# First attention of a two-block transformer on one core: joined maxima for one query tile in eight, outputs kept by channel, one bias product, a new opening

## The reference

```python
q = _rope(proj(Wq, bq)); k = _rope(proj(Wk, bk)); v = proj(Wv, bv)   # 16 heads of 16
scores = jnp.einsum('bhtd,bhsd->bhts', q, k) / scale                 # 2048 x 2048 a head
attn = jax.nn.softmax(scores, axis=-1)
out = jnp.einsum('bhts,bhsd->bhtd', attn, v)
out = out.transpose(0, 2, 1, 3).reshape(Bb, Tt, C)
return jnp.einsum('btc,oc->bto', out, Wo) + bo
```

## Time and profile before

| what | value |
|---|---|
| three runs | 3234.95 us median (3229.55 to 3236.52) |
| the profiled execution: span | 3219.8 us, 15.15 us under that median |
| PE busy | 3012.8 us (94%) |
| DVE busy | 2490.0 us (77%) |
| ACT busy | 2268.6 us (70%) |
| POOL busy | 780.4 us (24%) |
| mean granted PE clock | 0.964 |

### The profile page before, as it was taken

How to read it: one execution, slowest core, us unless ns; L and a number is a source line. 1 busy time by engine, 2 the same in 40 slices (tenths; PEclk the granted TensorE clock), 3 DMA queues, 4 the chain that set the end, 5 groups by cost and what they waited for, 6 DMA issues and landing times. The chain is left out here.

```text
span 3219.8 us, 63296 instructions
## 1 busy us (share of the span) xinstructions
PE 3012.8 (94%) x23672; PEld 1873.1 (58%) x23672; DVE 2490.0 (77%) x4820; ACT 2268.6 (70%) x4998; POOL 780.4 (24%) x1019
## 2 busy tenths in 40 slices
PE   8969999999999999999985999999999999999995
PEld 5733333333333333333354788888888888888884
DVE  4668899999989999899445767677777767777774
ACT  3407788888878888788875767676667767676663
POOL 4510000000000000000054434343434434343432
PEclk9958999999989999999997999999999999999998
DMA  3333212333322233322040000000000000000002
GB/s 115 112 82 41 38 25 41 41 41 41 41 32 32 40 41 41 41 41 41 12 161 23 1 1 0 0 0 0 0 1 35 1 1 0 0 0 0 0 1 71
DMA packets 47115, 99.37 MB, mean 31 GB/s; under 512 B 17184, under 2 KB 29472, under 8 KB 40480
## 3 DMA queue, kind: packets, MB, share of 16 engines
q1 hardware_dynamic: 42400, 95.48, 15.6%
q10 hardware_dynamic: 4544, 1.38, 0.2%
HBM read 71.13 MB, written 25.69 MB: 30 GB/s over the span
## 5 line engine op out<-in xcount | busy, mean ns | idle before, releaser
L691 DVE TENSOR_REDUCE mx<-aux 128x1 f32<-128x1024 f32 x1024 | 1246.5, 1224 | 116.4 <-PE aux L556 108.8
L661 ACT ACTIVATE probs<-scores 128x512 f32<-128x512 f32 x2048 | 1118.5, 597 | 250.1 <-PE scores L580 143.2
L556 PE MATMUL aux<-k_stack,q_stack 48*128 48x512 f32 x2048 | 792.8, 466 | 27.7 <-DMA k_stack<-qk_dram 19.5
L580 PE MATMUL scores<-q_stack,k_stack 50*128 50x512 f32 x2048 | 777.8, 456 | 13.4 <-ACT probs L661 13.4
L592 PE MATMUL pv<-probs,v_ones 128*32 128x256 f32 x8192 | 670.2, 400 | 0.1
L580 PEld LDWEIGHTS scores<-q_stack,k_stack 50*128 50x128 f32 x2048 | 317.3, 189 | 439.5 <-ACT probs L661 414.7
L592 PEld LDWEIGHTS pv<-probs,v_ones 128*32 128x32 f32 x8192 | 162.8, 109 | 373.6 <-ACT probs L661 275.8
L556 PEld LDWEIGHTS aux<-k_stack,q_stack 48*128 48x128 f32 x2048 | 320.5, 194 | 77.7 <-DVE mx L691 51.7
L522 POOL CAST m_parts<-head_max 128x16 fp32r<-128x16 f32 x32 | 6.3, 198 | 1355.9 <-DVE head_max L696 1355.9
L1241 PE MATMUL bank<-QO,w_sb 128*128 128x128 f32 x2816 | 328.2, 277 | 1.5 <-ACT QO L1328 1.5
L1241 PEld LDWEIGHTS bank<-QO,w_sb 128*128 128x128 f32 x2816 | 322.5, 193 | 2.5 <-ACT QO L1328 2.5
(11 more groups left out here) (175 smaller groups left out, 4628.2 us busy)
## 6 DMA issues: line engine op xcount, KB each, us to landing
q_stack<-qk_dram SPq DMA_DIRECT2D x192, 128.0 KB, 5.2
k_stack<-qk_dram SPq DMA_DIRECT2D x192, 128.0 KB, 6.8
qk_dram<-qkT_hi SPq DMA_DIRECT2D x32, 256.0 KB, 3.1
qk_dram<-qkT_lo SPq DMA_DIRECT2D x32, 256.0 KB, 3.6
out<-x_sb SPq DMA_DIRECT2D x9, 384.0 KB, 4.0
wqkv_sb<-in_wqkv SPq DMA_DIRECT2D x2, 1536.0 KB, 7.7
w_sb<-in_w SPq DMA_DIRECT2D x2, 1408.0 KB, 11.7
x_sb<-in_x SPq DMA_DIRECT2D x1, 2048.0 KB, 18.9
```

Of the source, the lines that this page charges most:

```text
L556: last = nc.tensor.matmul(aux[:, ring["unit"], block_of_keys % 2], q_stack[rows, r % BODY, tile * P:(tile + 1) * P], k_stack[rows, r % BOD ...
L580: nc.tensor.matmul(scores[:, item % BANKS1], k_stack[0:SCORE_ROWS, r % BODY, s * P:(s + 1) * P], q_stack[0:SCORE_ROWS, r % BODY, j * 512:( ...
L661: nc.scalar.activation(probs[:, item % PROBS], scores[:, item % BANKS1], ACT.Exp, scale=float(D1) ** -0.5).then_inc(probs_ready, 1)
L691: nc.vector.reduce_max(mx[:, slot, tile, half:half + 1], aux[:, unit].rearrange("p a k -> p (a k)"), AX.X).then_inc(max_taken, 1)
```

## The change

1. Projection: the two one-row bias products become one product of 128 rows. `picked` is zero but for rows 0 and 32, which are one; `bias_parts` holds the high part of the bias, and in rows 32 to 63 the low part.
2. Attention, maxima: in the last of each eight query tiles, and in all 24 tiles of the new opening, the four blocks of keys are joined in pairs. PE makes the difference of two blocks in PSUM (one product with q, one with minus q, made by POOL into `q_minus`), ACT takes its positive part into `excess` (Relu), and DVE adds it to the lower blocks and takes the maximum in one instruction (`tensor_tensor_reduce` over 1024). The difference goes through the same three banks as the scores. All other tiles are as before.
3. Attention, order: all engines' lists are unrolled. The maxima run 24 tiles ahead. The maximum rows are copied by DVE, and go to `q_stack` by DMA without DRAM.
4. Attention, outputs: `pv` is copied by ACT and moved by eight DMAs a head into `outputs` and `totals`, both by channel. After every eight heads DVE inverts `totals` (four times 128x512) and POOL multiplies.
5. Output: no transposes; Wo is multiplied from `outputs` directly. Tiles go in pairs, the addition of x is on POOL, over both tiles of a pair.

The feed-forward code changes only in where `kT` lies. The diff, cut to its core:

```diff
-                        for n, part in enumerate((bias_hi, bias_lo)):
-                            nc.tensor.matmul(out, ones_row[0:1, :], part[0:1, columns], start=(n == 0), stop=False)
+                        nc.tensor.matmul(out, picked[:], bias_parts[:, columns], start=True, stop=False)
...
+SPAN = TB // 2
+AHEAD = 3
+OPENING = AHEAD * SPAN
+JOINED = {16: 0, 23: 1}
+CHUNK = 8
...
+            for n, start, stop in Q_MINUS_PIECES:
+                pool.wait_ge(for_max_loaded[n], 16 * LOADS)
+                nc.gpsimd.tensor_scalar(q_minus_first[max_rows, n * TB + start:n * TB + stop], q_stack[max_rows, n, start * P:stop * P].rearrange("p (t c) -> p t c", c=P).bitcast(F32),
+                                        -1.0, None, ALU.mult).then_inc(q_minus_made, 1)
...
+            def difference(t, k, out):
...
+                nc.tensor.matmul(out, q_stack[max_rows, n % BODY, tile * P:(tile + 1) * P], k_stack[max_rows, n % BODY, (2 + k) * 512:(3 + k) * 512], start=True, stop=False)
+                nc.tensor.matmul(out, minus, k_stack[max_rows, n % BODY, k * 512:(k + 1) * 512], start=False, stop=True).then_inc(act_filled, 1)
...
+            for t in range(OPENING):
+                if t == FIRST_ROWS:
+                    maximum_rows(0)
+                for k in range(2):
+                    difference(t, k, for_act(2 * t + k))
+                for keys in range(2):
+                    for_dve(t, keys)
...
+                nc.scalar.activation(excess[:, number % 2, k], scores[:, item % BANKS1], ACT.Relu).then_inc(act_emptied, 1)
...
+                nc.vector.tensor_tensor_reduce(out=above, in0=aux[:, unit % 2].rearrange("p a k -> p (a k)"), in1=above, scale=1.0, scalar=LOWEST,
+                                               op0=ALU.add, op1=ALU.max, accum_out=mx[:, n % BODY, tile, 0:1]).then_inc(dve_emptied, 1)
...
+            def move_outputs(n):
+                c, place = n // CHUNK, n % CHUNK * D1
+                sp.wait_ge(pv_copied, n + 1)
...
+                for j in range(BLOCKS):
+                    for to, row in ((outputs[place:place + D1, c], VW * j), (totals[place:place + D1], VW * j + D1)):
+                        sp.dma_start(to[:, j * 512:(j + 1) * 512], o_stage[row:row + D1, n % 2]).then_inc(outputs_moved, 16)
...
+            def invert_totals(c, j):
+                dve.wait_ge(outputs_moved, 16 * 2 * BLOCKS * CHUNK * (c + 1))
+                here = totals[:, j * 512:(j + 1) * 512]
+                nc.vector.reciprocal(here, here).then_inc(inverted, 1)
...
+                    if p % 2 == 1 and i % SPAN == SPAN - 1 and n % CHUNK == 0 and n > 0:
+                        invert_totals(n // CHUNK - 1, i // SPAN)
+            for j in range(BLOCKS):
+                invert_totals(NH // CHUNK - 1, j)
...
-                    for k in range(NC):
-                        last = nc.tensor.transpose(psT[:, s, k * P:(k + 1) * P], o_tile[:, s, k * P:(k + 1) * P], ident[:])
...
+                        last = nc.tensor.matmul(psY[:, v % 4, i], outputs[:, b * NC + k, t * P:(t + 1) * P], w_sb[:, k], start=False, stop=(k == NC - 1))
...
+                if exists(t - 1):
+                    v = t - 1
+                    pool.wait_ge(y_normed_made, 2 * v + 2)
+                    nc.gpsimd.tensor_tensor(out=x1_sb[:, pair(v)], in0=y_normed[:, v % 2], in1=x_sb[:, pair(v)], op=ALU.add).then_inc(x1_made, 1)
```

More of the change, by code:

```diff
@@ new lines, in join_number, with rows_here, order_of_blocks @@
+        def join_number(t):
+            return t if t < OPENING else OPENING + (t - OPENING) // SPAN
+        def rows_here(p, i):
+            return p % 2 == 1 and i == ROWS_SLOT and p // 2 + 1 < NH
+        def order_of_blocks():
+            order, blocks = {}, iter([(t, k) for t in range(SPAN) for k in range(BLOCKS if t < SPAN - 1 else 2)])
+            for i in range(SLOTS):
+                order[i] = ("join", JOINED[i]) if i in JOINED else next(blocks)
+            return order
+        block_at = order_of_blocks()
@@ new lines, in _ @@
+            load(0, SECOND, for_max_loaded)
+            load(1, SECOND, for_max_loaded)
+            sp.wait_ge(minus_ones_made, 1)
+            load(0, 0, for_scores_loaded)
+            load_rows(0)
+            for n in range(NH):
+                sp.wait_ge(head_begun, n + 1)
+                if n + 1 < NH:
+                    load(n + 1, 0, for_scores_loaded)
+                if n + 2 < NH:
+                    load(n + 2, SECOND, for_max_loaded)
+                if n >= 1:
+                    move_outputs(n - 1)
+                if n + 1 < NH:
+                    load_rows(n + 1)
@@ L504, in _ @@
+            move_outputs(NH - 1)
         @block.gpsimd
@@ new lines, in for_act, with for_dve @@
+            def for_act(item):
+                if item >= BANKS1:
+                    pe.wait_ge(act_emptied, item - BANKS1 + 1)
+                return scores[:, item % BANKS1]
+            def for_dve(t, keys):
+                unit = unit_of[t, keys // 2]
+                if keys % 2 == 0 and unit >= 2:
+                    pe.wait_ge(dve_emptied, unit - 1)
+                last = score_for_max(t, keys, aux[:, unit % 2, keys % 2])
+                if keys % 2 == 1:
+                    last.then_inc(dve_filled, 1)
@@ L595, in weigh @@
                     last.then_inc(pv_done, 1)
-            def weigh_earlier(r, d, s, back, half, left, first):
-                if s >= back:
-                    if left >= d:
-                        weigh(r + d, s - back, half)
-                elif not first:
-                    weigh(r + d - 1, TB + s - back, half)
-            def output_item(r):
-                pe.wait_ge(pv_copied, r + 1)
-                unit = ring_unit()
-                for c in range(4):
-                    last = nc.tensor.transpose(aux[:, unit, 0, c * P:(c + 1) * P], o_stage[:, c * P:(c + 1) * P], ident[:])
-                last.then_inc(max_in_psum, 1)
-                for_dve()
@@ L631, in head @@
-            def head(r, n, left):
-                if r == 0:
-                    ring.update(start, last=list(start["last"]))
-                for d, s in steps():
-                    step(r, d, s, left)
-            for m in range(AHEAD):
-                score_for_max(m // (BLOCKS * TB), m // BLOCKS % TB, m % BLOCKS)
-                if m == 2 * FIRST_ROWS - 1:
-                    maximum_rows(0)
-            for s in range(LEAD):
-                step(-1, 1, s, 2, first=True)
-            assert ring["item"] == PROLOGUE_ITEMS + 1
@@ L644, in _, with weigh_earlier @@
-            start = dict(ring, last=list(ring["last"]))
-            all_heads(pe, head, ((m_parts_made, 1), (v_made, 1), (pv_copied, 1), (probs_ready, BLOCKS * TB), (max_taken, DVE_ITEMS), (rows_freed, 1)),
-                      ((for_max_loaded, 16 * LOADS), (for_scores_loaded, 16 * LOADS), (rows_loaded, 16)), looped=False)
+            def weigh_earlier(step, back, half):
+                if step >= back and step - back < NH * TB:
+                    weigh((step - back) // TB, (step - back) % TB, half)
@@ L663, in head @@
-            def head(r, n, left):
-                for d, s in steps():
-                    for j in range(BLOCKS):
-                        if (d, s, j) == (1, 1, 1):
-                            act.wait_ge(pv_done, TB * (r + 1))
-                            nc.scalar.copy(o_stage[:], pv[:]).then_inc(pv_copied, 1)
-                        if (d, s, j) == (0, ROWS_STEP, 3) and left >= 1:
-                            place = [what[3] for what in aux_items(left)].index("rows")
-                            copy_rows(r + 1, (first_unit(left) + place) % UNITS)
-                        if left >= d:
-                            exponentiate(r + d, s, j)
@@ L709, in head @@
-            def head(r, n, left):
-                if r == 0:
-                    taken[0] = start
-                for at, (d, s, j, kind, what) in enumerate(aux_items(left)):
-                    unit = (first_unit(left) + at) % UNITS
-                    if kind == "max":
-                        take_max((r + what[0]) % BODY, what[1], what[2], unit)
-                    if kind == "out":
-                        write_output(r, n, unit)
-            units = [("max", u) for u in range((AHEAD + BLOCKS * LEAD) // 2)]
```

608 lines of the change are left out of this document (306 added, 302 removed).

## The result

| | median us (lowest to highest) | span of the profiled execution |
|---|---|---|
| before | 3235.73 (3229.55 to 3268.19) | 3219.8 |
| changed | 3507.39 (3469.86 to 3508.76) | 3507.0 (in all 3508.76; mean granted clock 0.886) |

What follows compares the result with a forecast made beforehand. PE was taken to bound projection and attention. Terms -37 (projection) -18 (opening) -37 (steady attention) +60 (inversions) +21 (end) -9 (output) = -20: span 3199.8, plus 15.15 to the median, 3215 us; range 3138 to 3262.

Steps and rivals of the forecast that it cites:

- Attention, the steady part: Heads of attention: 41.8 us each, 1.2 less, over 31 heads -37 us; bounds -55 and 0.
- The joins: Joined query tiles in attention heads: two extra products at slots 16 and 23 of each span, 0.93 us a head.
- Rival C: Attention: the joined tile makes ACT the bound, +47 us over 61 spans, 3262 us; chance 0.09.
- The inversions: Attention: 12 inversions of 3.7 us stall PE, 40 us, plus 20 of low clock: +60 us; bounds 0 and +75.
- rival A: Attention and its end: inversions are cheap, 0.7 us each, so the stalls go; 3143 us; chance 0.18.
- The projection: Projection phase: tile of 3.3 us instead of 4.21, with an earlier clock rise, -37 us; bounds -15 and -46.
- rival D: Projection: the shorter PE list uncovers the chain PE, ACT, DVE, POOL, DVE; -15 instead of -37, 3237 us; chance 0.08.
- The opening: Start of attention: 24 joined tiles in 38 us, clock rising after three tiles, -18 us; bounds -23 and +15.
- rival B: Opening and first projection tiles: clock stays at 1.2 GHz, opening +15, projection -28, 3257 us; chance 0.12.
- Rival E: Opening: weight loads not hidden, each of 144 products waits 0.11 us, adding 14 to 16 us; 3230 us; chance 0.03.
- End and output: Two terms: end of attention +21 us (bounds +8, +27); output phase -9 us (bounds -20, +12).
- What would show it wrong: Signs: PE waiting for `xT_lo`/`qk_rot` in projection or `excess`/`scores` at slots 16 and 23, or low clock in heads without inversions.

Runs made afterwards that it cites:

- aligned kernel: Changed kernel with only the weighings moved right behind the second product of a VectorE unit, inversions whole: 3260.3 us, 1.0104 of before.
- misplaced order with short inversions: Changed kernel, weighings left between a unit's two products, each inversion over 32 of its 512 columns: 3480.64 us, 1.0759 of before.
- warm opening: Changed kernel with 66 extra 128x128 products of the identity while PE would wait for its loads before the opening: 3470.26 us.

## Why the prediction was wrong, point by point

- **Attention, the steady part: the step that failed.** I wrote "A head: 39.5 + 0.9 + 1.4 = 41.8". It measured 45.98 at 2.4 GHz, and more in heads with low clock, which I expected only behind inversions. The 39.5 rests on the half step of before, of which I had said that DVE follows "with 0.1 us to spare". That spare time belongs to one order: both products of a unit between two weighings. I counted the instructions that the change adds and removes, and did not ask where the unchanged ones now stand to each other. The parity of AHEAD is in the diff. The term of -37 was +242 (-20 + 261.7) in the traces; with the order kept and short inversions it was -20. Of the 1.4 us that I kept for waits at heads, 40.53 - 39.5 = 1.0 remained, but the joins, next, cost 1.0 us a head more than I had put in.
- **The joins** I charged with 0.9 us a head for their products; with the wait for ACT's bank they cost 1.9. "Which gives nothing while PE bounds", of DVE's saved pass, was right. Rival C had the right engine and the wrong quantity: what delays PE is a wait for one of ACT's three banks at slot 25, not ACT's busy time.
- **The inversions**: 3.34 us each, 6.5 ns an element, against my 3.7; so rival A (0.7 us) falls. They cost +81 in heads with the weighings in the right place, against +60. The mechanism was right; the low clock behind a set was undersized. In the trace of the aligned kernel it lasted at least the 52 us from 590 to 642, where I took stretches of 20 from the earlier trace rows. The estimate of 4.3 us that I worked out from the repeat count of 8 in the Trainium skill ("VectorE: DVE Perf Modes", First, the fixed hardware budget) was too high against these 3.34 us.
- **The projection**: -50.9 for -37, beyond my bound of -46. 11 tiles fall in the first 37 us, against 5. Two starts of the new bias product give the tile:

```profile
16.00:53.00 37.00, 7.61 (x11) 1.00 0.35 108
```

```profile
90.83 0.47 PE L307 MATMUL psQK<-bqkv_parts,picked_rows 128*128 128x512 f32 x1
...
93.93 0.47 PE L307 MATMUL psQK<-bqkv_parts,picked_rows 128*128 128x512 f32 x1
```

  A tile takes 3.10 us, not 3.3. I had summed 3.26 and rounded up for a chain of waits that did not come (rival D). The sum itself missed 0.16: the first one-row product had also followed the transposes late (94.63 - 94.32 = 0.31 us in the trace of before, now 93.93 - 93.79 = 0.14). For 26 tiles that makes 26 x (4.21 - 3.10) = 29 us in place of 24. The other 22, for which I had 13, are the start: `qk_cos` (L243), once a tile, started 2.6, 2.7 and 3.3 us apart in the first tiles, so the two tiles at low clock that I had put there did not come.
- **The opening**: +10.4 for -18 (+12.4 by the forecast's own boundary). This is rival B's half: the clock stayed at 1.2 GHz with TensorE busy 58.2 of 60 us., on which I set the rise against it, are products of 128 rows in another phase. The joined maximum took 1.22 to 1.23 us against my 1.35. Rival E has no part: in the first 5.3 us of the warm opening, at full clock, the same products of 48 rows followed each other at 0.23 us (149.92 - 149.69), as I had priced them; at 1.2 GHz they take 0.43.
- **End and output**: +19.3 for +21, -11.8 for -9. Both terms held.
- **What would show it wrong** named waits for `excess` or `scores` at slots 16 and 23, and low clock in heads without an inversion. The second came, and of the first a wait for a bank of `scores` two slots behind the join; the wait behind the slow pace, on `aux` in every other half step, was not on my list.
- **The last step of the sum**: the 15.15 us added to the span were scatter (see the result), which does not bear on the miss of 292 us.

## What to carry to other kernels

Two engines that meet at double buffers and run within 10% of each other's pace, as here PE's 1.233 us and DVE's 1.13, can have their slack in one order of instructions only. When a change shifts one stream against another by a single place, work out again, for each buffer, when it is begun and when it was emptied; counts and busy times did not show it here. And price work that relieves an engine only when that engine bounds: here a relief of DVE was paid with PE's and ACT's time.

## What the runs showed of the hardware

- In the misplaced order with short inversions the granted clock was 0.71 over 405 us while PE's busy share read 99%. All 39 falls between first and last score in that trace and the changed kernel's stand beside a wait of TensorE of 0.65 us or more (three of them 2.61 us), once a head at most; waits of 0.3 us in every second half step ran through whole heads at 2.4 GHz. With the weighings moved the longest wait of TensorE in the heads, away from the inversions, was 0.2 us (but for 0.47 in the first step), and the granted clock was 1.00 in every window shown away from them. The busy share of a page does not warn of it; the starts of successive instructions do.
- A row of products of 48 rows without a gap did not keep the clock up: in the warm opening it fell at 153.0 us with TensorE busy 5.30 of 5.30 us before it, and in the changed kernel it stayed at 0.50 with 58.2 of 60 us busy.
- `RECIPROCAL` took 3343 ns for 128x512 and 943 for 128x128: at 128 partitions its time goes by the columns, so a chunk's totals cost 0.94 us packed on all partitions and 4 x 3.34 = 13.4 us repeated over 16 rows.
- Products on rows 0 to 31 and on rows 64 to 111 did not overlap in the opening, though scores (rows 0 to 49) and products for the maxima (rows 64 to 111) start within 0.01 us of each other in every half step. The extra ones were of plain float32 and 128 columns (two records each in the trace), the others of the rounded type and 512; which of these decides was not tried.
